# A Perceiver kernel of twelve stages: semaphores cleared behind one barrier instead of two, their numbers used again one stage later

## What is computed

```python
x = x + _L0_xattn_ref(ctx_1024, _layernorm(x, axis=-1), mask_BxS2_bk1, ...)   # masked attention, 8 heads
x = x + _L0_attn_ref(_layernorm(x, axis=-1), ...)                             # mLSTM, 8 heads
x = x + _L0_ffn_ref(_layernorm(x, axis=-1), ...)                              # experts, 2 of 8
x = x + _L1_xattn_ref(_layernorm(x, axis=-1), ctx_1024, ...)                  # attention, 16 heads
x = x + _L1_attn_ref(_layernorm(x, axis=-1), ...)                             # sums of exp of causal scores
x = x + _L1_ffn_ref(_layernorm(x, axis=-1), ...)                              # experts with a gated unit
x = x + _L2_xattn_ref(_layernorm(x, axis=-1), ctx_1024, ctx_1024, ...)        # one head
x = x + _L2_attn_ref(_layernorm(x, axis=-1), ...)                             # projection and MLP
x = x + _L2_ffn_ref(_layernorm(x, axis=-1), ...)                              # experts
x = x + _L3_xattn_ref(ctx_1024, _layernorm(x, axis=-1), ...)                  # 8 heads, rotary keys
x = x + _L3_attn_ref(_layernorm(x, axis=-1), ...)                             # latent attention, 16 heads
x = x + _L3_ffn_ref(_layernorm(x, axis=-1), ...)                              # gated recurrence, 32 steps
```

## Time and profile before

| | |
|---|---|
| median of 3 runs | 2846.2 us (2842.02 to 2846.78) |
| span of the profiled execution | 2841.0 us; the page gives no other time of it |
| TensorE matmuls busy | 2559.5 us, 90% |
| VectorE, ScalarE, GpSimd busy | 1786.9, 1631.6, 1403.1 us |
| mean granted TensorE clock | 0.939 |
| instructions | 43966 |

### The profile page before, as it was taken

One profiled execution on the slowest core, in us unless ns is written; L12 is line 12 of the kernel. 1 busy time (PEld: TensorE's weight loads), 2 busy tenths in 40 slices (PEclk: granted clock), 3 DMA queues, 4 the chain that ended last, 5 costly groups with the idle time before them and its releaser, 6 DMA issues. The chain is left out here.

```text
span 2841.0 us, 43966 instructions
## 1 busy us (share of the span) xinstructions
PE 2559.5 (90%) x16307; PEld 2149.4 (76%) x16307; DVE 1786.9 (63%) x3733; ACT 1631.6 (57%) x2865; POOL 1403.1 (49%) x1111
## 2 busy tenths in 40 slices
PE   5999999587999999999976898796999999999777
PEld 4899998376999999999965766594677777777547
DVE  7888874545555555555534544617888888888472
ACT  4888885335766666666633343433666666666333
POOL 1877875111766666666620052204766756666140
PEclk9999999789999999999986998798999999999885
DMA  3323231022011111111004041202000000000000
GB/s 111 97 81 107 80 86 37 14 57 62 24 42 29 36 36 36 36 36 36 13 6 133 1 117 30 60 1 79 25 13 24 13 24 25 13 25 2 3 1 8
DMA packets 222574, 117.83 MB, mean 41 GB/s; under 512 B 21368, under 2 KB 217632, under 8 KB 222368
## 3 DMA queue, kind: packets, MB, share of 16 engines
q1 hardware_dynamic: 222368, 115.11, 14.7%
HBM read 100.39 MB, written 13.64 MB: 40 GB/s over the span
## 5 line engine op out<-in xcount | busy, mean ns | idle before, releaser
L851 POOL TENSOR_TENSOR L_xattn_held<-L_xattn_held,L_xattn_shift 128x512 f32<-128x512 f32 (+1 forms) x613 | 763.0, 1291 | 286.0 <-ACT L_xattn_shift L772 285.9
L569 PEld LDWEIGHTS L_xattn_acc<-L_xattn_rows,L_xattn_held 128*128 128x128 f32 (+2 forms) x5120 | 618.4, 192 | 34.8 <-DVE L_xattn_mixed L954 9.2
L569 PE MATMUL L_xattn_acc<-L_xattn_rows,L_xattn_held 128*128 128x129 f32 (+2 forms) x5120 | 627.9, 275 | 5.5 <-DVE L_xattn_mixed L954 5.5
L975 DVE TENSOR_TENSOR L_xattn_running<-L_xattn_ring,L_xattn_running 128x512 f32<-128x512 f32 (+1 forms) x384 | 264.2, 688 | 270.0 <-PE L_xattn_ring L551 258.4
L762 ACT ACTIVATE L_xattn_held<-L_xattn_held 128x512 f32<-128x512 f32 (+2 forms) x640 | 400.4, 631 | 0.2
L1617 POOL TENSOR_TENSOR L_xattn_projected<-L_xattn_along,L_xattn_crossed 128x512 f32<-128x512 f32 (+1 forms) x256 | 271.5, 1072 | 256.0 <-DVE L_xattn_crossed L1684 254.0
L755 ACT COPY L_xattn_held<-L_xattn_ring 128x512 f32<-128x512 f32 (+1 forms) x416 | 243.3, 585 | 227.8 <-DVE L_xattn_running L975 193.2
L549 PE MATMUL L_xattn_ring<-L_xattn_queries_hi,L_xattn_keys_hi 128*128 128x512 f32 (+2 forms) x640 | 281.3, 440 | 3.4 <-DVE L_xattn_keys_lo L879 2.0
L551 PE MATMUL L_xattn_ring<-L_xattn_queries_hi,L_xattn_keys_lo 128*128 128x512 f32 (+2 forms) x640 | 253.7, 396 | 0.0
L550 PE MATMUL L_xattn_ring<-L_xattn_queries_lo,L_xattn_keys_hi 128*128 128x512 f32 (+2 forms) x640 | 253.1, 395 | 0.0
L1324 PE MATMUL L_xattn_sums<-L_xattn_probT,L_xattn_rows 128*128 128x256 f32 (+2 forms) x896 | 242.5, 382 | 0.6 <-ACT L_xattn_mixed L1506 0.6
(11 more groups left out here) (588 smaller groups left out, 4818.9 us busy)
## 6 DMA issues: line engine op xcount, KB each, us to landing
L_xattn_raw<-in_ctx SPq DMA_DIRECT2D x16, 768.0 KB
context_normalised<-L_xattn_fresh SPq DMA_DIRECT2D x16, 768.0 KB
L_xattn_rows<-context_normalised SPq DMA_DIRECT2D x16, 768.0 KB
first_loads_fresh<-in_ctx SPq DMA_DIRECT2D x16, 768.0 KB
L_xattn_rows<-in_ctx SPq DMA_DIRECT2D x16, 768.0 KB
opening_staged<-in_ctx SPq DMA_DIRECT2D x16, 768.0 KB
L_xattn_xhat<-context_normalised SPq DMA_DIRECT2D x16, 768.0 KB
L_ffn_w<-in_L_ffn_W SPq DMA_DIRECT2D x2, 896.0 KB, 5.4
```

What stands on the lines that cost most here:

```text
L569: mm = nc.tensor.matmul(acc[:, c // 2, c % 2 * WIDE:(c % 2 + 1) * WIDE], held[0:n, u % 2, k, c * P:(c + 1) * P], rows[0:n, b % 2, k, :], s ...
L851: nc.gpsimd.tensor_tensor(tile, tile, shift[0:keys_of_tile[k]], ALU.subtract).then_inc(shifted, 1)
L975: seen = nc.vector.tensor_tensor(most, bank, most, ALU.max)
```

## The change

`Stage.clear` no longer issues a barrier, and does nothing at all for a stage without semaphores. The clear on GpSimd stays where it was, behind the block's own barrier. The numbers of the cleared semaphores are held back in `Resting` and given out again only when one more block has been opened and a further `Stage` is made. So the stage right behind gets other numbers, and the barrier at the end of its block lies between a clear and the next use of the same number.

```diff
+class Resting:
+
+    def __init__(self):
+        self.blocks, self.sems = 0, []
+
+    def add(self, nc, sems):
+
+        nc.clear_and_free_semaphores(sems)
+        self.sems.append((self.blocks, [nc.alloc_semaphore(name=f"{h.name}_resting", num=h.num) for h in sems]))
+
+    def release(self, nc):
+
+        for at, sems in self.sems:
+            if at < self.blocks:
+                nc.extend_free_semaphores([h.num for h in sems])
+        self.sems = [(at, sems) for at, sems in self.sems if at >= self.blocks]
+
+
 class Stage:
 
+    resting = Resting()
 
     def __init__(self, nc, ctx, name):
         self.nc, self.ctx, self.name, self.sems = nc, ctx, name, []
+        self.resting.release(nc)
         ctx.callback(self.clear)
...
     def clear(self):
 
-        self.nc.clear_and_free_semaphores(self.sems)
-        self.nc.all_engine_barrier()
+        if self.sems:
+            self.resting.add(self.nc, self.sems)
 
     def block(self):
+        self.resting.blocks += 1
         return self.ctx.enter_context(self.nc.Block())
...
     with ExitStack() as ctx:
+        Stage.resting = Resting()
         s = Stage(nc, ctx, "all")
```

## The result

The changed kernel took 2832.14 us (median of 8 runs, 2826.79 to 2842.73) against 2842.87 us for the kernel before run beside it (8 runs, 2840.32 to 2847.92). The ratio is 0.9957, 95% interval [0.9945, 0.9969]. By the ratio that is 12 us of gain, between 9 and 16, where 10.4 were forecast; the two medians differ by 10.7. The time lies 3.7 us under the forecast of 2835.8. Of that 3.3 are the level: the kernel before is at 2842.87 us here and was at 2846.2 in the three runs that the forecast started from. The profiled execution took 2832.42 us with a span of 2830.6.

The account below looks back on a forecast made before the run. TensorE bounds the span, but at stage ends all engines stand still: 10.8 us of barriers, less 0.3 and 0.1, gives 10.4, taken from the 2846.2 us median: 2835.8 us, range 2831.5 to 2841.0.

Parts of the forecast that it names:

- What bounds those places: At stage ends every engine rests and no transfer is awaited, so each gap on the path is worth its whole length.
- The price of a round: At the stage-end barriers, one plain round was taken to cost 0.33 us.
- Both sums: Barrier time over the whole kernel, from SyncE's waits and from idle times at the boundaries: 10.8 us each way.
- The correction of -0.3: At 1934 us VectorE leaves the block's own barrier late; the others' 0.3 us wait was expected to stay.
- GpSimd without cover: GpSimd's clear makes it start stages about 0.26 us later; mostly covered, with 0.1 us lost at most in the tenth.
- Numbers that rest: Held-back semaphore numbers may split a range clear in two, between 0 and 0.45 us on GpSimd; taken as 0.
- The clock: At two low-clock starts, 0.9 us of the won time might come back; whole gain taken, 0.9 kept for the range.
- The level: The runs' median, 2846.2 us, lies 5.2 above the 2841.0 us span; the gain was taken from the median.
- The range: For the changed kernel's median time, 2831.5 to 2841.0 us, with 2 in 10 outside.
- rivals 2 and 3: Clock at stage starts: 2, half the gain is lost, 2841.0 us, chance 0.12; 3, it rises later, 2853.8 us, 0.05.

Follow-up runs that it names:

- e7: The changed kernel with twenty small memsets and drains on VectorE behind each clear, so that VectorE enters stages late; 2906.31 us.
- e1: The kernel before with nine barriers instead of one behind each stage's clear; 2915.76 us, ratio 1.0243.
- e3: The changed kernel with each clear done twelve times over, so that GpSimd enters stages late; 2840.49 us.
- e9: The changed kernel with the two barriers put back in front of the eighth stage alone; 2838.61 us, ratio 0.9978.
- e14: The changed kernel with one plain barrier in front of the eighth stage; 2838.73 us (one run).
- e15: The kernel before's barriers everywhere except in front of the eighth stage, numbers resting as in the changed kernel; 2840.36 us, ratio 0.9982.
- e12: The changed kernel with three plain barriers put back in front of the seventh stage; 2830.44 us (one run).
- e2: The kernel before with clear and barrier left out only for the six stage objects that own no semaphore; ratio 0.999.

## Why the prediction was right or wrong

- **What bounds those places** was right. Gaps in which all engines stand still are worth their whole length: e7 priced VectorE's lateness at nearly one for one over the whole kernel, though not in each stage.
- **The price of a round** was right in kind; 0.33 us by two pairs of releases, and 0.33 for most plain rounds of e1, 0.35 in the mean with the slower ones. Both sums gave 10.8 us, the traces 10.7.
- **The correction of -0.3** for VectorE's late release at 1934 us was wrong. GpSimd was clearing in that time, and nobody would have gone on earlier: the gap shrank by 0.93 us there (1.31 to 0.38), not by the 0.7 forecast. The wait had a second owner, and I subtracted it once too often.
- **GpSimd without cover** was right as a whole (e3) and mis-sized at one place. I gave the tenth stage a loss of 0.1 us; its first matmul lost the whole 0.93. I had put its 0.22 us wait for the gains down as slack beside a path through VectorE. It was the sign that the loads were the path: once VectorE came earlier by more than they did, the wait grew to 1.08 us, and to 0.83 and 1.93 in the other two traces. The second stage gave 0.62 of its 0.75 us, since GpSimd's second memset came to lie beside VectorE's normalised tile, whose first four operations took 1.25 us in place of 1.12.
- **Numbers that rest** cost what I took, near nothing, though five more clears stand in the trace.
- **The clock** is the step that failed. I asked only at which clock the won time is worked, took the whole gain, and kept 0.9 us of loss for the range. What the clock does later in a stage was put at nothing, and the rivals that name it both had it take time. In truth the barriers in front of the eighth stage cost 5.4 us through it: e9 and e14 put them back, e15 takes them away in the kernel before. About half of the measured 12 us comes from one gap of 1.26 us. The stage spent 41.9, 38.6 and 41.9 us at 1.2 GHz in the three traces before and 23.9, 27.3 and 23.9 in those of the changed kernel. The row that I had for this place, 1.00 in the first 3.3 us, was true and too short; the next 30 us show 0.51. That the gate's observation isn't restarted by the kernel's work (the Trainium skill, page "TensorE: Matmul & The Clock Gate", Part 1: The HAM clock gate) is neither confirmed nor refuted here: e12, which was to shift the start without a gap, was swallowed by the seventh stage.
- **The level.** I took the 5.2 us between span and median as what lies around a span. It isn't: the changed kernel's profiled execution took 2832.42 with a span of 2830.6, the third trace of the kernel before 2846.02 with 2844.1. Less than 2 us lie around in each. With as much around it, the execution behind the 2841.0 us span took about 2843 us (an estimate), which is the kernel's median of 2842.87 in the later measurement; the 2846.2 of the first three runs was high.
- **The range** held the median by 0.6 us at its low end. It was too narrow for a wrong reason: three runs within 4.8 us. Eight of the changed kernel spread over 16 us, from 2826.79 to 2842.73, and the first stage alone (504 to 511 us from release to release in the six unaltered traces) accounts for up to 7 of them.
- **The sum** 10.7 - 0.9 (tenth stage) + 5.4 (eighth) = 15.2 is above the 12.2 measured and within its interval. The difference is the tenth and the eleventh stage, which are longer in the means (1.7 and 1.35 us more than their gaps let expect) but scatter by 2 us between traces of the same kernel. Their time at 1.2 GHz grew with them: behind the last release 27.1, 33.8 and 34.0 us before and 34.9, 38.9 and 35.6 after in the tenth, 34.1, 43.9 and 43.8 before and 43.9, 44.4 and 40.6 after in the eleventh. What makes it grow, and whether the change does, is open; rivals 2 and 3 may have come true in part there, but no run shows it.
- **Luck.** That 10.4 us came so close to 10.7 (medians) and 12 (ratio) is luck: the sum left out 5.4 us of gain in the eighth stage and about 4 us of loss in the tenth and the eleventh, and these nearly cancel.

## What to carry to other kernels

Count the barriers that stand between stages and look at which owner needs them; a rest of one stage for the numbers replaces a second meeting of the engines, and an empty stage needs none. Price them by the idle time of the engine that leads the next stage, then look at the loads of each stage's start: where an engine already waits a little for one, earlier compute only waits longer. And read the granted clock for tens of us behind every gap that changes, not only for the first few: here one barrier, 0.7 us of gap, in front of a stage made it 5 us longer. One trace isn't enough for that: e2 shows the short form behind a gap of 1.26 us.

## What the runs showed of the hardware that I had not expected

- The granted clock of one stage has two courses. With 0.3 us of gap in front of it, it is 0.72 to 0.77 in the 30 us that begin 5.3 us into the stage; with one or two barriers more it is 0.50 to 0.56 in five traces of six and 0.72 in the sixth (e2). The stage takes 59 or 64 us. Both begin with 5.3 us at 1.00.
- Four operations of VectorE (128 x 128, f32) took 2.14 us while GpSimd ran one TENSOR_TENSOR of 1.26 us, and 1.12 us without it.
- A plain barrier round lasts 0.33 us in most places, even nine behind each other, and 0.35 in the mean of 176 (e1); a round with a clear in it is longer, since it waits for GpSimd: 0.72 us in e14.
- The landing of the tenth stage's last gain differs by about 1 us between executions of one program: TensorE's first matmul came at 9.93, 9.68 and 10.79 us in the three traces of the changed kernel.
